# Sums of squares over a head: one plain fp32 matmul instead of an fp32r one and a bf16 one

## The reference, cut to what matters

```python
def l2norm(t):
    return t / jnp.maximum(jnp.linalg.norm(t, axis=-1, keepdims=True), 1e-12)

def attn_layer(x, Wqkv, qs, ksc, Wo):
    q, k, v = jnp.split(x @ Wqkv, 3, -1)          # 16 heads of 64
    q = l2norm(q) * qs
    k = l2norm(k) * ksc
    q = q * cos * scale + rotate_half(q) * sin * scale
    k = k * cos * inv + rotate_half(k) * sin * inv
    return local_attention(q, k, v) @ Wo          # window 32, softmax

for i in range(6):
    x = attn_layer(shift_tokens(x), ...) + x
    x = ffn_layer(shift_tokens(x), ...) + x
```

## Time and profile before

| What | Value |
|---|---|
| Runs, median (lowest to highest) | 5195.39 us (5191.45 to 5198.09), 3 runs |
| Span of the profiled execution | 5196.3 us |
| TensorE matmuls busy | 4059.5 us (78%) |
| VectorE busy | 4157.5 us (80%) |
| ScalarE busy | 2852.2 us (55%) |
| GpSimd busy | 2552.5 us (49%) |
| Mean granted TensorE clock | 0.919 of full speed |

### The profile page before, as it was taken

One profiled execution on the slowest core, in us unless ns is written; L12 is line 12 of the kernel. 1 busy time (PEld: TensorE's weight loads), 2 busy tenths in 40 slices (PEclk: granted clock), 3 DMA queues, 4 the chain that ended last, 5 costly groups with the idle time before them and its releaser, 6 DMA issues. The chain is left out here.

```text
span 5196.3 us, 147973 instructions
## 1 busy us (share of the span) xinstructions
PE 4059.5 (78%) x62298; PEld 2893.8 (56%) x63066; DVE 4157.5 (80%) x6032; ACT 2852.2 (55%) x4736; POOL 2552.5 (49%) x1604
## 2 busy tenths in 40 slices
PE   2012048999979999789999789999799997899996
PEld 2011036666656666566666566666566665666664
DVE  5977978888878888778888788888788887788885
ACT  1011036666656666556666566666566665565665
POOL 3665844544435544445455445445355444454542
PEclk8566579999989999999999999999899999999998
DMA  0000011111111111111111111111111111111112
GB/s 21 0 6 6 0 43 37 25 25 25 25 45 25 25 25 25 33 37 25 25 25 25 33 37 25 25 25 25 46 25 25 25 25 33 37 25 25 25 25 57
DMA packets 86314, 139.19 MB, mean 27 GB/s; under 512 B 14457, under 2 KB 35600, under 8 KB 83984
## 3 DMA queue, kind: packets, MB, share of 16 engines
q1 hardware_dynamic: 78698, 127.06, 9.3%
q10 hardware_dynamic: 6950, 2.39, 0.2%
HBM read 30.59 MB, written 4.46 MB: 7 GB/s over the span
## 5 line engine op out<-in xcount | busy, mean ns | idle before, releaser
L1054 POOL TENSOR_TENSOR kn<-kn,r 128x512 f32<-128x512 f32 x385 | 495.6, 1287 | 1659.0 <-ACT r L968 1659.0
L960 ACT ACTIVATE sq<-ps 128x512 f32<-128x512 f32 x768 | 459.3, 598 | 905.8 <-PE ps L784 901.7
L1090 DVE TENSOR_TENSOR rb<-ps,tab 128x512 f32<-128x512 f32 x768 | 527.7, 687 | 404.7 <-PE ps L784 346.1
L966 ACT ACTIVATE r<-r 128x512 f32<-128x512 f32 x769 | 485.7, 632 | 567.3 <-DVE r L1101 566.7
L1054 POOL TENSOR_TENSOR qn<-qn,r 128x512 f32<-128x512 f32 x384 | 495.4, 1290 | 550.0 <-ACT r L968 550.0
L1047 POOL TENSOR_TENSOR kn<-ra,rb 128x512 f32<-128x512 f32 x384 | 631.2, 1644 | 79.7 <-DVE ra L1092 70.2
L1094 DVE TENSOR_TENSOR sqlo<-sq 128x512 fp32r<-128x512 f32 x768 | 644.9, 840 | 0.0
L782 PE MATMUL ps<-xhs,wl 128*128 128x512 f32 x768 | 403.5, 525 | 237.3 <-PEq L122 178.5
L1101 DVE TENSOR_SCALAR r<-ps 128x512 f32<-128x512 f32 x768 | 524.2, 683 | 29.0 <-remote 10.5
L1047 POOL TENSOR_TENSOR qn<-ra,rb 128x512 f32<-128x512 f32 x384 | 537.6, 1400 | 0.0
L857 PEld LDWEIGHTS ps<-v,pt 64*32 64x32 f32 x24768 | 394.2, 108 | 243.7 <-issue 186.9
(11 more groups left out here) (182 smaller groups left out, 9161.1 us busy)
## 6 DMA issues: line engine op xcount, KB each, us to landing
v<-v SPq DMA_DIRECT2D x96, 768.0 KB, 5.8
v<-v SPq DMA_DIRECT2D x96, 192.0 KB, 5.7
raw<-in_L_ffn_Wqkv SPq DMA_DIRECT2D x7, 1536.0 KB, 7.3
tab<-in_rotary SPq DMA_DIRECT2D x6, 1024.0 KB, 5.7
raw<-in_L_ffn_Wo SPq DMA_DIRECT2D x6, 512.0 KB
sT<-so ACTq DMA_DIRECT2D x3, 768.0 KB, 3.3
xnat<-in_L_attn_hidden_states SPq DMA_DIRECT2D x8, 256.0 KB, 3.4
srow<-sT SPq DMA_DIRECT2D x8, 256.0 KB, 3.1
```

Source lines behind the costliest of these rows:

```text
L960: nc.scalar.activation(sq[:, k, :], ps[:, A, :], ACT.Square).then_inc(cur["sq"], 1)
L966: nc.scalar.activation(r1[:, k, :], r1[:, k, :], ACT.Ln, scale=RN * RN).then_inc(cur["ln"], 1)
L1054: nc.gpsimd.tensor_tensor(dst, dst, r1[:, k, :], ALU.mult).then_inc(cur["qkn"], 1)
L1090: nc.vector.tensor_tensor(rb[:, k, :], ps[:, BB, :], tab[:, 2 * k + 1, :], ALU.mult)
```

## The change

The squares go to TensorE as they are, in fp32, with the 0/1 matrix read in fp32 from the constants. `sqlo`, its semaphore `sl` and the two converted copies of the matrix are gone, and `squares` waits for `sq`, which ScalarE signals. Nothing else changes its place in any engine's order: per round, VectorE's list loses 16 subtractions and TensorE's has 16 matmul statements where it had 32. A plain fp32 matmul statement shows in the trace as two MATMUL records, an fp32r or bf16 one as one; the records of L799's matmuls are missing from the trace, those of its weight loads are there.

```diff
@@ -576,7 +573,7 @@
-    names = ("xh v vev ab sq sl rot g ssq r ln add qkn S m sub exp rs ri pt ptev o oev ot otev wo x1 "
+    names = ("xh v vev ab sq rot g ssq r ln add qkn S m sub exp rs ri pt ptev o oev ot otev wo x1 "
@@ -646,9 +643,7 @@
-            nc.vector.tensor_copy(pairr[:], con[:, C_PAIR:C_PAIR + P]).then_inc(s_hi, 1)
-            nc.vector.tensor_copy(pairb[:], con[:, C_PAIR:C_PAIR + P]).then_inc(s_hi, 1)
-            dve.wait_ge(s_hi, 7)
+            dve.wait_ge(s_hi, 5)
@@ -793,11 +788,10 @@
             def squares(i, k):

-                pe.wait_ge(cur["sl"], 2 * i + k + 1)
+                pe.wait_ge(cur["sq"], 2 * i + k + 1)
                 after(pe, "g", 2 * i + k)
-                nc.tensor.matmul(ps[:, SS, :], pairr[:], sqlo[:, k, :], start=True, stop=False)
-                nc.tensor.matmul(ps[:, SS, :], pairb[:], sq[:, k, :].bitcast(BF16)[:, 1::2],
-                                 start=False, stop=True).then_inc(cur["ssq"], 1)
+                nc.tensor.matmul(ps[:, SS, :], con[:, C_PAIR:C_PAIR + P], sq[:, k, :],
+                                 start=True, stop=True).then_inc(cur["ssq"], 1)
@@ -1090,9 +1084,6 @@
                 nc.vector.tensor_tensor(rb[:, k, :], ps[:, BB, :], tab[:, 2 * k + 1, :], ALU.mult)
                 dve.wait_ge(cur["sq"], 2 * i + k + 1)
                 nc.vector.tensor_tensor(ra[:, k, :], ps[:, A, :], tab[:, 2 * k, :], ALU.mult).then_inc(cur["rot"], 1)
-                after(dve, "ssq", 2 * i + k - 1)
-                nc.vector.tensor_tensor(sqlo[:, k, :], sq[:, k, :], sq[:, k, :].bitcast(BF16)[:, 1::2],
-                                        ALU.subtract).then_inc(cur["sl"], 1)
```

More of the change, by code:

```diff
@@ L544, in transformer @@
     identb = sb("identb", [P, P], BF16)
-    pairr = sb("pairr", [P, P], F32R)
-    pairb = sb("pairb", [P, P], BF16)
     xhs, xls = sb("xhs", [P, 2, S], F32R), sb("xls", [P, 2, S], F32R)
@@ L549, in transformer @@
     sq = sb("sq", [P, 2, S])
-    sqlo = sb("sqlo", [P, 2, S], F32R)
     r1 = sb("r1", [P, 2, S])
```

## The result

The changed kernel takes 5205.1 us (median of 20 runs) against 5197.6 us before (20 runs). The ratio is 1.0016, with a 95% interval from 1.0009 to 1.0022: some 8 us slower, where 99 were forecast. The profiled execution has a span of 5208.5 us, 12 more than before, at nearly the same mean clock (0.921).

The account below looks back on a forecast made before the run. The prediction took TensorE's own stream to set the pace: 5196.3 + 300 for the fp32 squares - 201 of returned waits = 5295 us profiled, so 5294 against 5195.4, 1.9% slower; range 5215 to 5355.

Parts of the forecast that it names:

- The price on TensorE: At the 768 squares, one fp32 matmul for the old pair adds 0.38 us (0.40 in first halves): +300 us, bounds 230 and 330.
- Guard, 146.0 us: TensorE's listed wait at the second sum of squares: VectorE comes earlier without the subtraction, so all 146 us go.
- in pair 3 nothing is waited for: In pair 3 TensorE was taken as unheld, so its spacings gave the old pair's price: 0.56 us from square to next matmul.
- 242 us in all: TensorE's listed waits for VectorE and GpSimd at five places: 146.0 second sum of squares, 34.3 `fl`, 34.1 `gated`, 15.9 `kn`, 11.3 `ra`.
- `fl`*: all goes: TensorE's wait for `fl`, behind the guard on VectorE: it comes 0.6 us earlier, so all 29 us come back.
- `gated`: TensorE's wait for `gated`, 34.1 us, 0.71 each: it comes 0.60 earlier, 29 us come back, 0.11 each is left.
- `ra`: TensorE's wait at a round's start, 11.3 us in 24 places: 0.30 of 0.47 us each goes, 7 us back.
- `kn` in pair 6: TensorE's wait at `scores` for GpSimd's `kn`: the 0.30 us wait grows by 0.20 in 48 places, 10 us lost.
- the guard that doesn't come free: Rival: a later first square holds the guard past TensorE's arrival, the 146 us stay: 5440 us, half of them 5367; chance 0.06.
- the 0.08 that vanishes: Rival: the 0.08 us wait for the square's weights disappears, so a square adds +0.30 us: 5224 us; chance 0.14.
- Same: Rival: the 0.08 us weight wait vanishes and all 242 us of waits go: 5183 us, or within 10 of before; chance 0.07.
- Fp32 at half rate: Rival: a 512-column fp32 statement costs one record, 0.43 us, under the old 0.48: 4956 us, faster; chance 0.03.

Follow-up runs that it names:

- Run 1: Kernel before without the subtraction, both matmuls kept, low parts of the squares left out: 4994.0 against 5214.4 us, ratio 0.9576.
- run 4: Kernel before with plain fp32 for the queries (first square of a pair) alone, keys keeping split and subtraction: 5212.5 against 5198.0 us, ratio 1.0028.
- e7_sqlo_from_psum: Kernel before, keys' subtraction taking one input from PSUM and writing an unread tile, keys' low parts left out: 5085.9 against 5198.0 us, ratio 0.9781.

## Why the prediction was wrong

**The price on TensorE was right.** Forecast were 300 us. The first halves cost 148.2 (the table's second row). For the second halves the unheld spacing to the square went from 0.41 to 0.49, and from there the fifth row's unheld spacing grew by 0.31, together 0.39 x 384 = 150. That makes 298.

**The failed step is "Guard, 146.0 us"**, and behind it the sentence that in pair 3 nothing is waited for. The mechanism was right: all of the hold went, and there was slack. Its size was read from a list that leaves out what lies under the recorded tail of the transposes, 0.23 us in each held pair (0.64 - 0.41), and all of the hold where it is not longer than that (pairs 3 and 7). It measured 228 us, 82 more. Run 1 shows it, and run 4 agrees; the list alone could not. The same error lies in "242 us in all" and in "nearly all that VectorE can give back".

**Three smaller steps failed too.** The first is "*`fl`*: all goes". The list says so (34.3 to 5.1), but by spacing `fl` gave back 13 us and not 29. In pair 4 these rows of VectorE and TensorE, before and after, show why:

```profile
2433.68 1.16 DVE L1168 TENSOR_TENSOR fl<-fc,fh 128x512 fp32r<-128x512 f32 x1
...
2434.98 0.47 PE L782 MATMUL ps<-fh,w1l 128*128 128x512 f32 x1 [0.61 <-DVE fl L1168]
```

```profile
2439.11 1.38 DVE L1159 TENSOR_TENSOR fl<-fc,fh 128x512 fp32r<-128x512 f32 x1
...
2439.53 1.02 PE L793 MATMUL ps<-sq,con 128*128 128x512 f32 x2
...
2440.64 0.47 PE L777 MATMUL ps<-fh,w1l 128*128 128x512 f32 x1
```

Both times the matmul starts 0.14 to 0.15 us after `fl` ends, just as the held squares start 0.14 after the guard. In the changed kernel the hold lies under the square's record, which ends at 2439.53 + 1.02 = 2440.55, and is not listed. `fl` also takes longer there, 1.38 us and not 1.16. Pair 5 has the same 15 matmuls behind its square and no `fl`: there the spacing to `values` is 4.12 before and 4.42 after, in pair 4 it is 4.72 and 4.76. So `fl` held by 0.60 and still holds by 0.34.

The second is that the sum has no term for the turns of the loop. The five waits were those for VectorE and GpSimd, and the pause called "issue" was put at nothing without a reason. It gave back 17 us by spacing (15 in the list). Why it got shorter is open.

The third is the hidden part of other waits. In pair 0 `kn` held `scores` by up to 0.2 us, which the list leaves out; it gave back 5 us (19.6 to 14.9 in the spacing ahead of `scores`). `gated` gave back 0.60 in each of 48 pairs 6 (3.51 to 2.91 in the spacing ahead of the transposes), 29 us as forecast, but 2.91 is 0.34 over the unheld 2.57, not the 0.11 forecast.

`ra` gave back 8 where 7 were forecast, `kn` in pair 6 took 10 as forecast. So: 298 - 228 - 29 - 17 - 13 - 8 - 5 + 10 = 8 us, against 8 in the table and 8 in the medians. Of the 91 us between forecast and result, 82 are the guard's hold and 17 the turns of the loop; the 16 that `fl` kept point the other way.

**The rivals.** Neither the guard that doesn't come free nor the 0.08 that vanishes happened. "Same" gave nearly the time that was measured, for reasons that were not the true ones: a square costs 0.39, not 0.30, and the waits were worth more than 242. That is luck, and no support for it. The break-even stood at 201 / 768 = 0.26 us a square; with what really came back it is 290 / 768 = 0.38, just under the price of 298 / 768 = 0.39. Fp32 at half rate is excluded by the 0.86 us of each square.

**The signs asked for** came, in the main: 1536 records (0.86 us to the next matmul and 0.08 ahead of the start, for the 0.93 to 0.96 asked for), the guard waiting for TensorE in 337 places, `kn` at 0.51 us in pair 6, GpSimd's sum near that for the queries (1.276 against 1.334 us). `gated` is not listed, and holds by 0.34 in place of 0.1. VectorE's busy time fell by 553 us and not 645, mostly since neighbouring records overlap by some 0.08 us; TensorE's rose by 268, where 250 were expected and L799's matmuls had been missing before.

## What to carry to other kernels

A wait that a trace lists on TensorE starts at a modelled end; measure it as the spacing of starts less the same spacing where nothing holds, and look for a place that surely is unheld before calling one so. Do the same for a wait that has gone from the list: `fl` had gone from it and still held. Price a change from a table of such spacings, place by place, and it also shows where to make the change: here six of eight places, keys only, gained 2.4% where all sixteen halves lost 0.2%. A wait that goes often moves to the next one on the same path, as `fl` and `kn` did. A pause that the list gives to no engine can move as well, as the one at the turns of the loop did.

## What the runs showed of the hardware

A VectorE subtraction of 128x512 with both inputs in SBUF took 0.68 us alone and up to 1.675 us beside GpSimd's additions, of which those for the keys took 1.64 us on the mean, and 1.28 in the changed kernel; with one input from PSUM it took 0.68 us also where GpSimd's addition for the queries lay over all of it (`e7_sqlo_from_psum`). Not each meeting stretches VectorE: in pairs 3, 4 and 7 of the kernel before, `sqlo` overlapped the addition for the keys and kept its 0.68 us, and the addition took 1.65. A run whose trace has the bf16 matmul's records shows the old pair directly (`e7_sqlo_from_psum`, TensorE): 0.32 us to the second record and 0.24 for its streaming.

```profile
2404.94 0.48 PE L799 MATMUL ps<-sqlo,pairr 128*128 128x512 f32 x1
2405.26 0.40 PE L800 MATMUL ps<-sq,pairb 128*128 128x512 bf16 x1
2405.50 0.38 PE L813 MATMUL ps<-maskb,identb 128*128 128x256 bf16 x2
```
